# Routed experts of a decoder layer: every token times all experts, against slots sorted by expert in DRAM

## The chip, the core and the metric

The kernel runs on one core of one Trainium2 chip, in one launch. The metric is the device time of that core in microseconds (us), lower is better. The profile calls TensorE PE (its weight loads PEld), VectorE DVE, ScalarE ACT, GpSimd POOL and the queue that issues most DMAs SP.

## What is computed

2048 tokens (16 tiles of 128) of width 256 pass causal self-attention, cross-attention and a feed-forward stage, each behind a layer norm and added to `x`. Only the last stage changes. Its core, cut:

```python
shared = _swiglu(flat @ w_in.T) @ w_out.T                 # hidden width 512
g_idx = jnp.argmax(g_probs, axis=-1)                      # one of 2 groups of 4 experts
masked = jnp.where(g_idx[:, None] == egid[None, :], e_logits, -jnp.inf)
p_expert = _softmax(masked) * g_prob
topv, topi = jax.lax.top_k(p_expert, 2)                   # 2 of 8 experts for each token
w_se = zeros((S, 8)).at[arange(S)[:, None], topi].add(topv)
h = _swiglu(flat @ w1.T)                                  # the same h for all experts
routed = 0
for e in range(8):
    routed = routed + h * w_se[:, e:e + 1] @ w2[e].T      # 512 -> 256 for each expert
out = x + shared + routed
```

## The kernel before

All products are float32 by three matmuls of halves rounded to float32r (`product`, lines 118 to 124): high by low, high by high, low by high, summed in PSUM. So each operand exists as `_hi` (made by ACT with a copy) and `_lo` (the rest, by DVE or POOL: `weights_lo_pool`). The weights come through three staging buffers `stage`, loaded by SP; a load waits until the `_lo` of the piece three before it is done.

Two blocks follow each other, with a barrier of all engines between them. The first holds both attentions. The second is the feed-forward stage, over four groups of four token tiles (`TPG`), a rolled loop from the second on. For each group, TensorE does: `gate_logits`; `hidden(g)`, eight units of 12 matmuls of 512 columns (four for `w1`, four for `win`; "unit" below), the first four with hidden rows on the partitions, so that they can be the weights side later; and `outputs(g)`: for each token tile four chunks (two experts each, 12 matmuls of 512 columns), that is every token times all eight experts, and one chunk `wout` (12 matmuls of 256 columns). ACT makes silu and the high halves, DVE the product `h` with the gate half and the low halves, and in `combine` the weighted sum over the experts with the weights `wse` of `gating(g)` (zero for the six not chosen). `combine` follows the matmuls chunk by chunk through four PSUM banks `OB`; a finished tile goes out by one DMA.

```python
for c in range(OUTS):                       # 5 chunks: 4 pairs of experts, 1 shared
    ...
    for k in range(HT):
        ...
        mm = product(dst, lhs, rhs, k == 0, k == HT - 1)
    mm.then_inc(out_mm, 1)
```

## Time and profile before

| | |
|---|---|
| median of 3 runs | 955.28 us (953.64 to 955.29) |
| profiled execution, first to last instruction | 953.4 us |
| TensorE busy | 929.8 us, 98% |
| second block (feed-forward), from about | 649.3 us |
| its TensorE busy time to the end | 294.65 of 304.1 us |
| granted TensorE clock, mean | 0.996 |

The profiled execution has no time of its own beside its span; the median of the runs is 1.9 us above that span. Times in the rows are us from the span's start, durations of one instruction are in ns where a row says mean. The program's own copy of the line numbers is used: L122 to L124 are the three matmuls of `product`, so groups are told apart by their tiles.

### The profile page before, as it was taken

How to read it: one execution, taken by the hardware profiler on the slowest of the kernel's cores; microseconds unless marked ns; L12 is line 12 of the kernel's file. 1: busy time of each engine (PE TensorE's matmuls, PEld its weight loads, DVE VectorE, ACT ScalarE, POOL GpSimd, SP SyncE). 2: the span in 40 equal slices, each digit the busy share in tenths (PEclk: the TensorE clock that was granted, in tenths of full speed). 3: DMA queues.
4: the chain of work that ended last, by engine and by line, in shares of the span. 5: the costliest groups of instructions: out<-in, count | busy, mean ns of one | idle time of the engine just before them, and what ended most of it. 6: DMA issues, size and time to landing. Idle time of an engine off the chain costs nothing. (4 is left out here: it accounts for less than half of the span.)

```text
span 953.4 us, 17962 instructions
## 1 busy us (share of the span) xinstructions
PE 929.8 (98%) x6242; PEld 798.4 (84%) x6242; DVE 629.0 (66%) x1630; ACT 518.1 (54%) x1603; POOL 231.4 (24%) x243
## 2 busy tenths in 40 slices
PE   7999999999999989999999999997999999999998
PEld 5788889888888878988988988886788888888887
DVE  5787778687688777767667766766843653553543
ACT  4876677667667767766766777776301400400400
POOL 0443124124115344512421522435000000000000
PEclk9999999999999999999999999999999999999999
DMA  7200000000001020000000020112000000000000
GB/s 230 102 23 2 1 0 0 0 0 0 0 1 46 23 67 2 23 2 0 0 22 0 0 88 0 46 45 103 8 12 12 0 11 11 0 11 11 1 11 12
DMA packets 13184, 22.07 MB, mean 23 GB/s; under 512 B 1108, under 2 KB 7764, under 8 KB 12628
## 3 DMA queue, kind: packets, MB, share of 16 engines
q1 hardware_dynamic: 13140, 21.51, 6.9%
q8 instruction: 25, 0.41, 0.2%
q14 instruction: 19, 0.16, 0.1%
HBM read 19.41 MB, written 2.10 MB: 23 GB/s over the span
## 5 line engine op out<-in xcount | busy, mean ns | idle before, releaser
L383 POOL TENSOR_TENSOR prob<-prob,rsum 128x512 f32<-128x512 f32 x128 | 133.2, 1040 | 395.2 <-DVE rsum L576 395.2
L461 ACT ACTIVATE prob<-psS,nmin 128x128 f32<-128x128 f32 x512 | 180.9, 377 | 6.1 <-DVE nmin L560 3.5
L444 ACT ACTIVATE pT_hi<-psT 128x512 fp32r<-128x512 f32 x128 | 69.5, 595 | 85.9 <-PE psT L715 85.9
L461 ACT ACTIVATION_READ_ACCUMULATOR prob<-psS,nmin 128x1 f32 x512 | 111.6, 218 | 0.0
L545 DVE TENSOR_TENSOR oT_lo<-psT,oT_hi 64x512 fp32r<-64x512 f32 x128 | 88.0, 688 | 22.5 <-ACT oT_hi L449 20.5
L539 DVE TENSOR_TENSOR pT_lo<-psT,pT_hi 128x512 fp32r<-128x512 f32 x128 | 82.1, 682 | 1.6 <-ACT pT_hi L444 1.4
L449 ACT ACTIVATE oT_hi<-psT 64x512 fp32r<-64x512 f32 x128 | 75.8, 592 | 5.2 <-PE psT L124 3.6
L533 DVE TENSOR_TENSOR v_lo<-psW,v_hi 128x512 fp32r<-128x512 f32 x64 | 44.2, 690 | 50.5 <-ACT v_hi L439 50.5
L122 PE MATMUL psT<-pT_lo,v_hi 128*128 128x256 f32 x256 | 72.8, 284 | 4.6 <-DVE pT_lo L539 4.6
L439 ACT ACTIVATE v_hi<-psW 128x512 fp32r<-128x512 f32 x64 | 38.2, 597 | 68.5 <-PE psW L124 68.5
L703 PE MATMUL psS<-kt_lo,q_hi 64*128 64x128 f32 x512 | 73.7, 285 | 0.0
L122 PE MATMUL psA<-wo_lo,oT_hi 128*128 128x256 f32 x256 | 72.8, 284 | 0.8 <-DVE oT_lo L545 0.8
L124 PE MATMUL psT<-pT_hi,v_lo 128*128 128x256 f32 x256 | 72.6, 283 | 0.0
L123 PE MATMUL psA<-wo_hi,oT_hi 128*128 128x256 f32 x256 | 72.4, 283 | 0.0
L123 PE MATMUL psT<-pT_hi,v_hi 128*128 128x256 f32 x256 | 72.3, 283 | 0.0
L124 PE MATMUL psA<-wo_hi,oT_lo 128*128 128x256 f32 x256 | 72.2, 282 | 0.0
L560 DVE CUSTOM_DVE_ANT_0 psS<-psS,mask 128x128 f32<-128x128 f32 x256 | 65.4, 325 | 9.1 <-PE psS L703 8.6
L715 PE MATMUL psT<-ident,prob 128*128 128x128 f32 x512 | 69.9, 280 | 0.8 <-DVE oT_lo L545 0.8
L703 PE MATMUL psS<-kt_hi,q_lo 64*128 64x128 f32 x512 | 70.4, 272 | 0.0
L703 PE MATMUL psS<-kt_hi,q_hi 64*128 64x128 f32 x512 | 70.3, 271 | 0.0
L703 PEld LDWEIGHTS psS<-kt_lo,q_hi 64*128 64x128 f32 x512 | 48.6, 187 | 17.9 <-issue 15.7
L576 DVE RECIPROCAL rsum<-psums 128x4 f32<-128x4 f32 x128 | 22.0, 172 | 57.3 <-ACT prob L461 57.3
(196 smaller groups left out, 2595.0 us busy)
## 6 DMA issues: line engine op xcount, KB each, us to landing
stage<-w SPq DMA_DIRECT2D x4, 1024.0 KB, 4.8
stage<-ctxT SPq DMA_DIRECT2D x4, 512.0 KB, 4.1
out<-fin SPq DMA_DIRECT2D x16, 128.0 KB, 1.7
xres<-x SPq DMA_DIRECT2D x3, 512.0 KB, 8.3
stage<-wq SPq DMA_DIRECT2D x2, 512.0 KB, 5.3
stage<-wk SPq DMA_DIRECT2D x2, 512.0 KB, 6.6
stage<-wv SPq DMA_DIRECT2D x2, 512.0 KB, 5.4
stage<-wr SPq DMA_DIRECT2D x2, 512.0 KB, 5.0
```

The costliest lines, as they stand in the source:

```text
L122: nc.tensor.matmul(o, lh, rl, start=start, stop=False, **kw)
L123: nc.tensor.matmul(o, lh, rh, start=False, stop=False, **kw)
L124: return nc.tensor.matmul(o, ll, rh, start=False, stop=stop, **kw)
L383: nc.gpsimd.tensor_tensor(prob[:, r, :], prob[:, r, :], rsum[:, r].unsqueeze(2).broadcast_to([P, TPG, P]), ALU.mult).then_inc(prob_done, 1)
L444: nc.scalar.activation(pT[0][:, i, :], psT[:, i, :], ACT.Copy).then_inc(pT_hi, 1)
L449: nc.scalar.activation(oT[0][r, parity, :, :], banks(psT)[r, :, h, :], ACT.Copy).then_inc(oT_hi, 1)
L461: e = nc.scalar.activation(prob[:, n, :], flat(psS[:])[:, n * P:(n + 1) * P], ACT.Exp, bias=nmin[:, n:n + 1], scale=-1.0, accum_out=psums[ ...
L539: nc.vector.tensor_tensor(pT[1][:, i, :], psT[:, i, :], pT[0][:, i, :].bitcast(F32), ALU.subtract).then_inc(pT_lo, 1)
L545: nc.vector.tensor_tensor(oT[1][r, parity, :, :], banks(psT)[r, :, h, :], oT[0][r, parity, :, :].bitcast(F32), ALU.subtract).then_inc(oT_l ...
L560: m = nc.vector.tensor_tensor_reduce(sc, sc, mask[:], 1.0, LARGE, ALU.add, ALU.min, nmin[:, i * TPG + n:i * TPG + n + 1])
L703: mm = nc.tensor.matmul(psS[:, h, c], lhs[r, c], rhs[r, c], start=n == 0, stop=n == 2, skip_group_check=True)
L715: mm = nc.tensor.transpose(psT[:, i, n * P:(n + 1) * P], prob[:, i * TPG + n, :], ident[:])
```

## The change

The 2048 tokens times 2 choices are sorted by expert. A slot is a row of a DRAM tensor `hs` (4992 rows of 512 float32); each expert owns whole tiles of 128 slots, so there are at most `NT` = 39 tiles, and each has one expert.

- The `w1` units are now made by token tile with the token on the partition (units `H0` to `H15`, again 12 matmuls of 512 columns each), and `h` stays in the staging buffers. The `win` units are `S00` to `S33`. Both use the PSUM pairs `psS` and `psT` in turn; unit u waits until DVE has done unit u-2.
- The gate weights are worked out for groups 0 to 2 together and then for group 3 (`gate_maxima`, `gate_ranks`). `slot_counts` (17 small matmuls) and `slots` give each token its two slots; `slot_experts` gives each tile its expert.
- POOL issues 32 indirect DMAs that scatter `h` (128 rows of 2 KB each) to `hs`. `hs` is set to zero in the first block by one DMA of 10.2 MB. SP waits for all scatters and loads the tiles back, six in flight.
- For each of the 39 tiles TensorE transposes 128x512 (`turn`), ACT and DVE make the halves, TensorE loads the expert's column offset into a register (`value_load`) and does 12 matmuls of 256 columns (`expert`); ACT copies the result and SP writes it to `ys`.
- When all of `ys` is written, POOL issues 32 indirect DMAs that gather 128 rows of 1 KB each, through twelve buffers, and DVE adds them with their weights to `xres` (`add_routed`), which goes out.
- Order on TensorE: `H` and `S0` units with gates in between, the other `H`, `S10` to `S13`, `S20`, `shared_out(1)`, the 39 tiles, then `S21` to `S33` with `shared_out(2)`, at last `shared_out(3)`.
- The six late weight pieces of up to 1 MB are now ten: `w2` comes in eight of 512 KB, seven of whose low halves POOL makes.

```diff
+NT = (CHOICES * B * S + NE * (P - 1)) // P
+LOADS = 6
+YGS = 12
+BUFS = 3
...
+                sp.dma_start(hs.rearrange("(t p) d -> p t d", p=P),
+                             zero[:].unsqueeze(1).broadcast_to([P, NT, HID])).then_inc(slots_zero, 16)
...
             @block2.sync
...
+                for n in range(REUSED):
+                    sp.wait_ge(scattered[n], 2 * CHOICES * 16)
+                sp.wait_ge(scattered_rest, (HSLOTS - REUSED) * CHOICES * 16)
+
+                def load_slots(i):
+                    if i >= LOADS:
+                        sp.wait_ge(hT_mm, i - LOADS + 1)
+                    sp.dma_start(hl(i), hs[i * P:(i + 1) * P, :]).then_inc(hl_in[i % LOADS], 16)
+
+                for i in range(LOADS):
+                    load_slots(i)
+                for i in range(NT):
+                    if i + LOADS < NT:
+                        load_slots(i + LOADS)
+                    sp.wait_ge(y_copied, i + 1)
+                    sp.dma_start(ys[i * P:(i + 1) * P, :], y_rows(i)).then_inc(y_out[i % BUFS], 16)
...
             @block2.gpsimd
...
+                late_lo(LATE.index("win"))
+                ln_scale(pool, L0 + 2)
...
+                pool.wait_ge(slots_zero, 16)
+                pool.wait_ge(slots_known, 1)
+                for T in range(B):
+                    u = UNITS.index(f"H{T}")
+                    pool.wait_ge(h_done, u + 1)
+                    for c in range(CHOICES):
+                        d = nc.gpsimd.indirect_dma_start(
+                            hs[:, :], bass.IndirectOffsetOnAxis(ap=slot[:, c, T:T + 1], axis=0), h_slot(T), None,
+                            bounds_check=SLOTS - 1, oob_is_err=False)
...
+                for b in range(BUFS):
+                    pool.wait_ge(y_out[b], (NT // BUFS) * 16)
+                for n in range(B * CHOICES):
+                    if n >= YGS:
+                        pool.wait_ge(added, n - YGS + 1)
+                    nc.gpsimd.indirect_dma_start(
...
             @block2.scalar
...
+                def expert_hi(i):
+                    act.wait_ge(hT_mm, i + 1)
+                    if i >= BUFS:
+                        act.wait_ge(y_mm, i - BUFS + 1)
+                    nc.scalar.activation(flat(hT(0, i)), T_BANKS[i % BUFS], ACT.Copy).then_inc(hT_hi, 1)
+
+                def copy_rows(i):
+                    act.wait_ge(y_mm, i + 1)
...
+                    nc.scalar.activation(y_rows(i), Y_BANKS[i % BUFS], ACT.Copy).then_inc(y_copied, 1)
...
             @block2.vector
...
+                for i in range(NT):
+                    dve.wait_ge(hT_hi, i + 1)
+                    nc.vector.tensor_tensor(flat(hT(1, i)), T_BANKS[i % BUFS], flat(hT(0, i)).bitcast(F32),
+                                            ALU.subtract).then_inc(hT_lo, 1)
...
+                def add_routed(T):
+                    dve.wait_ge(shared_added, 2 * (T // TPG + 1))
+                    for c in range(CHOICES):
+                        n = T * CHOICES + c
+                        dve.wait_ge(yg_in[n % YGS], 16 * (n // YGS + 1))
...
+                        nc.vector.scalar_tensor_tensor(xres[:, T, :], yg(n), weight[:, c, T:T + 1], xres[:, T, :],
+                                                       ALU.mult, ALU.add).then_inc(added, 1)
...
             @block2.tensor
...
+                def turn(i):
+                    pe.wait_ge(hl_in[i % LOADS], 16 * (i // LOADS + 1))
...
+                    for k in range(HT):
+                        tr = nc.tensor.transpose(T_BANKS[i % BUFS][:, k * P:(k + 1) * P], hl(i)[:, k * P:(k + 1) * P], ident[:])
+                    tr.then_inc(hT_mm, 1)
+
+                def expert(i):
+                    offset = pe.value_load(offsets[0:1, i:i + 1], min_val=0, max_val=(NE - 1) * D)
+                    pe.wait_ge(hT_lo, i + 1)
...
+                    for k in range(HT):
+                        mm = product(Y_BANKS[i % BUFS], (hT(0, i)[:, k, :], hT(1, i)[:, k, :]),
+                                     tuple(w[:, k, bass.ds(offset, D)] for w in w2s), k == 0, k == HT - 1)
+                    mm.then_inc(y_mm, 1)
...
+                turn(0)
+                turn(1)
+                for i in range(NT):
+                    if i + 2 < NT:
+                        turn(i + 2)
+                    expert(i)
```

TensorE, before: the end of one token tile of `outputs`. The first three rows are the last products with a pair of experts, 512 columns; the next three begin the shared part, 256 columns.

```order
L122 MATMUL psT<-w2_lo,hid_hi 128x512
L123 MATMUL psT<-w2_hi,hid_hi 128x512
L124 MATMUL psT<-w2_hi,hid_lo 128x512
L122 MATMUL psA<-wout_lo,hid_hi 128x256
L123 MATMUL psA<-wout_hi,hid_hi 128x256
L124 MATMUL psA<-wout_hi,hid_lo 128x256
```

TensorE, after the change: the end of `shared_out(1)` and the first expert tile (`stage` holds the loaded slots, `w1_hi` and `w1_lo` hold the halves of the transposed rows).

```order
L143 MATMUL psA<-wout_hi,hid_lo 128x256
L1478 MATMUL psS<-ident,stage 128x128 x8
L1478 MATMUL psW<-ident,stage 128x128 x4
L1482 TENSOR_LOAD offsets
L1482 ISA x2
L141 ISA
L141 MATMUL psT<-w2_lo,w1_hi 128x256
L142 REGISTER_ALU
L142 MATMUL psT<-w2_hi,w1_hi 128x256
L143 MATMUL psT<-w2_hi,w1_lo 128x256
```

The 48 matmuls of 512 columns for each token tile are gone; in their place stand, 39 times, 4 transposes, one register load with 10 register instructions (the last five rows come four times), and 12 matmuls of 256 columns.

POOL, before, from its first low half in the second block to the end; its last three instructions are a loop over the layer norms.

```order
L257 TENSOR_TENSOR win_lo<-stage,win_hi 128x2048
L257 TENSOR_TENSOR w2_lo<-stage,w2_hi 128x2048 x2
L883 UNCONDITIONAL_BRANCH
L883 ISA
L150 TENSOR_TENSOR veps<-mv,eps 128x4
L152 TENSOR_TENSOR rstd<-veps,mhalf 128x4
```

POOL, after the change, from the same place (`wq_lo` is where the low half of `win` now goes) to the end.

```order
L277 TENSOR_TENSOR wq_lo<-stage,wq_hi 128x2048
L169 TENSOR_TENSOR veps<-mv,eps 128x4
L171 TENSOR_TENSOR rstd<-veps,mhalf 128x4
L277 TENSOR_TENSOR w2_lo<-stage,w2_hi 128x1024 x2
L169 TENSOR_TENSOR veps<-mv,eps 128x4
L171 TENSOR_TENSOR rstd<-veps,mhalf 128x4
L277 TENSOR_TENSOR w2_lo<-stage,w2_hi 128x1024 x5
L1012 DMA hs<-stage,slot 4992x512 x32
L1022 DMA stage<-ys,slot 128x256 x32
```

POOL, which had nothing to do behind its low halves but four small operations for each layer norm, now ends with 64 DMAs that it issues itself.

DVE, before: the end of its program, the last token tile of `combine`.

```order
L1022 SCALAR_TENSOR_TENSOR fin<-psA,wse,fin 128x256
L1022 SCALAR_TENSOR_TENSOR acc<-psA,wse,acc 128x256
L1026 TENSOR_TENSOR acc<-psA,acc 128x256
L1029 TENSOR_TENSOR fin<-fin,acc 128x256
```

DVE, after the change: the end of its program, from the last unit on.

```order
L1223 TENSOR_TENSOR silu<-psT,silu 128x512
L1228 TENSOR_TENSOR hid_lo<-silu,hid_hi 128x512 x2
L1366 SCALAR_TENSOR_TENSOR xres<-stage,weight,xres 128x256 x16
L1341 TENSOR_TENSOR xres<-psA,xres 128x512 x4
L1366 SCALAR_TENSOR_TENSOR xres<-stage,weight,xres 128x256 x16
```

All 32 additions of expert results now stand behind the last unit of the shared part.

## Rows read from the trace of the kernel before

**Rows 1.** The page, span and busy time of each engine.

```profile
span 953.4 us, 17962 instructions
PE 929.8 (98%) x6242; PEld 798.4 (84%) x6242; DVE 629.0 (66%) x1630; ACT 518.1 (54%) x1603; POOL 231.4 (24%) x243
```

**Rows 2.** Windows of the second block: busy of each engine, clock, DMA share, GB/s.

```profile
649.30:677.70 28.40, 22.22 (x88) 17.11 (x89) 23.48 (x20) 18.64 (x20) 14.36 (x5) 0.94 0.26 93
677.70:728.00 50.30, 50.30 (x250) 42.68 (x249) 27.56 (x76) 5.64 (x8) 1.21 (x2) 1.00 0.03 9
...
sum 304.10, PE 294.65 PEld 243.47 DVE 158.48 ACT 62.03 POOL 17.98; mean PE 36.83 PEld 30.43 DVE 19.81 ACT 7.75 POOL 2.25
```

**Rows 3.** Timeline of PE: start, length, instruction; from one token tile.

```profile
702.40 0.40 PE L122 MATMUL psA<-w_lo,hid_hi 128*128 128x512 f32 x1
...
713.30 0.28 PE L122 MATMUL psA<-wout_lo,hid_hi 128*128 128x256 f32 x1
...
714.74 1.04 PE L172 MATMUL psS<-ident,z 128*128 128x128 f32 x8
715.53 0.48 PE L122 MATMUL psA<-w_lo,hid_hi 128*128 128x512 f32 x1
```

**Rows 4.** Timeline of PE, two pieces of a score step with 64x128 matmuls.

```profile
212.39 0.27 PE L703 MATMUL psS<-kt_hi,q_lo 64*128 64x128 f32 x2
212.50 0.27 PE L703 MATMUL psS<-kt_lo,q_hi 64*128 64x128 f32 x2
```

**Rows 5.** Groups of instructions from 660 us on: count, busy, mean ns.

```profile
L1022 DVE SCALAR_TENSOR_TENSOR fin<-psA,wse,fin 128x256 f32<-128x256 f32 x24 | 11.6, 482 | 30.3 <-PE psA L124 30.2
L992 DVE TENSOR_TENSOR h<-psS,silu 128x512 f32<-128x512 f32 x15 | 10.4, 692 | 19.2 <-ACT silu L896 19.0
L896 ACT ACTIVATE silu<-psW 128x512 f32<-128x512 f32 x15 | 9.0, 599 | 23.6 <-PE psW L124 23.6
L152 POOL TENSOR_TENSOR rstd<-veps,mhalf 128x4 f32<-128x4 f32 x3 | 3.0, 1007 | 0.2
```

**Rows 6.** Timelines of POOL and DVE while the weights come in.

```profile
655.84 4.62 POOL L257 TENSOR_TENSOR w_lo<-stage,w_hi 128x2048 fp32r<-128x2048 f32 x1
656.02 4.99 DVE L1002 TENSOR_TENSOR hid_lo<-h,hid_hi 128x512 fp32r<-128x512 f32 x1
664.52 0.68 DVE L992 TENSOR_TENSOR h<-psW,silu 128x512 f32<-128x512 f32 x1
```

**Rows 7.** DMAs: size and median us from issue to landing; SP's issues at the start.

```profile
out<-fin SPq DMA_DIRECT2D x16, 128.0 KB, 1.7
xres<-x SPq DMA_DIRECT2D x4, 128.0 KB, 2.2
0.82 1.83 SPq L338 DMA_DIRECT2D xres<-x  x4
```

**Rows 8.** Window in which weights load: DMA share and GB/s are the last two columns.

```profile
655.00:660.00 5.00, 5.00 (x23) 3.89 (x21) 4.59 (x2) 3.71 (x5) 5.00 (x2) 1.00 0.55 210
```

**Rows 9.** Timeline of DVE, the gate weights of the first group, first and last.

```profile
680.55 0.16 DVE L939 TENSOR_REDUCE gmax<-logits 128x4 f32<-128x8 f32 x1
...
683.18 0.43 DVE L965 TENSOR_TENSOR above<-probs 128x256 f32<-128x256 f32 x1
...
685.35 0.19 DVE L976 SCALAR_TENSOR_TENSOR wse<-rank,probs 128x32 f32<-128x32 f32 x1
```

**Rows 10.** Windows of gaps in TensorE's work; the clock is third from the end.

```profile
665.00:670.00 5.00, 3.06 (x12) 2.18 (x12) 4.90 (x3) 3.52 (x4) 4.07 (x1) 1.00 0.31 105
670.00:675.00 5.00, 4.53 (x13) 3.58 (x14) 4.50 (x5) 0.63 (x1) 0.00 (x0) 0.66 0.00 0
```

**Rows 11.** The end, by timelines: last instruction of PE, DVE and SP.

```profile
949.86 0.28 PE L124 MATMUL psA<-wout_hi,hid_lo 128*128 128x256 f32 x1
950.63 0.42 DVE L1029 TENSOR_TENSOR fin<-fin,acc 128x256 f32<-128x256 f32 x1
951.23 0.33 SPq L870 DMA_DIRECT2D out<-fin  x1
```

More of the change, by code:

```diff
@@ new lines, in build, with s_before @@
+            ROUND = (range(0, 3 * TPG), range(3 * TPG, B))
+            UNITS = ["H0", "H1", "H2", "H3", "S00", "S01", "S02", "S03", "H4", "H5", "H6", "H7", "H8", "H9", "H10", "H11",
+                     "H12", "H13", "H14", "H15", "S10", "S11", "S12", "S13", "S20", "S21", "S22", "S23",
+                     "S30", "S31", "S32", "S33"]
+            S_UNITS = [n for n in UNITS if n[0] == "S"]
+            H_AFTER = ("w1 lower", "w1 upper", "win", "w2 2 upper", "w2 3 lower", "w2 3 upper")
+            def s_before(u):
+                return sum(n[0] == "S" for n in UNITS[:u])
@@ new lines, in _ @@
+                late_hi(4)
+                late_hi(5)
+                exps(0)
+                bias(3)
+                unit(9)
+                late_hi(6)
+                late_hi(7)
+                exps(1)
+                unit(10)
+                late_hi(8)
+                late_hi(9)
+                for u in range(11, UNITS.index("S10") + 1):
+                    unit(u)
+                for m in range(HT):
+                    unit(UNITS.index(f"S1{m}") + 1)
+                    split(f"S1{m}")
```

747 lines of the change are left out of this document (492 added, 255 removed).

## The prediction

> **What bounds the kernel now.** I read the page first, then windows over the second block, then TensorE's timeline inside a token tile, then the timelines of POOL and DVE where weights load. TensorE is busy for 98% of the span, DVE for 66%, POOL for 24% [rows 1]. In the second block TensorE works 294.65 of 304.1 us [rows 2], so the reader should see that this stage is bound by the number of matmul columns alone. The idle 9.4 us are in the first group (28.4 us, 22.2 busy) and behind the last matmul. Within a token tile the rows follow each other without a gap: from the first product with an expert pair to the first shared one 10.90 us pass for 48 matmuls of 512 columns, 0.227 us each; the 12 of 256 columns take 1.44 us, and 8 transposes 0.79 us [rows 3]. DVE keeps up with room to spare: in the steady window it is busy 27.6 of 50.3 us.
>
> **What is removed.** The experts' products: 16 tiles times 10.90 us = 174.4 us, all on the path.
>
> **What is added on TensorE.** Each of the 39 expert tiles has 12 matmuls of 256 columns (1.44) and 4 transposes (half of 0.79, so 0.40): 1.84 us, 71.8 in all. The 32 units, the 16 shared products, the gate products and the transposes of z are as many as before, only in another order. The 17 small matmuls of the slot counts are about 0.1 each by the transposes, less than 2 us with the first one's wait: I take 1. If nothing ever waits, the span is 953.4 - 174.4 + 71.8 + 1 = 851.8 us. Everything else is what has to be given back.
>
> **The register load in each expert tile.** The trace has no load of a register on TensorE. It blocks TensorE's sequencer, with 10 register instructions behind it. What hides it is that the sequencer runs ahead: matmuls of 128 columns are issued each 0.055 us (two in 0.11 [rows 4]), while one of 256 columns lasts 0.12, so a tile lets it gain 12 times 0.065 plus a little on the transposes, about 1.0 us. Against that stand the register instructions, at 0.05 each by the same row 0.5 us, and the load. Lower bound: all hidden, 0. Upper bound: the nearest round trip through memory in the trace, a small store's 1.7 us [rows 7], gives 0.5 + 1.7 - 1.0 = 1.2 us for a tile, 47 in all. Between them I take 0.4 for a tile, that is a load of 0.9, shorter than a DMA because nothing is written: +15.6 us. The Trainium skill, DMA: Bandwidth & Descriptors, in Latency and other measured facts, gives a floor of about 600 ns for such a load. As an estimate by that page the loop would give back 39 times 0.1, some 4 us; no row here shows it.
>
> ACT and DVE don't bind the loop: ACT has a copy of 512 columns, 0.6 us, and one of 256, DVE one low half read from PSUM, 0.69 like the product [rows 5], against 1.84 to 2.3. The pair runs two tiles ahead, 3.7 us, and takes about 1.6. The DMAs have 256 KB in and 128 KB out for a tile. At a DMA share of 0.55 the trace moved 210 GB/s [rows 8], so about 380 GB/s is there, and 393 kB need 1.0 us. They are hidden too, by the same 1.84 us.
>
> **The scatters.** The price of one indirect DMA on POOL, c, is the term that decides, and the trace has none: POOL issues no DMA there. Lower bound: SP issues one of 128 rows in 1.83 / 4 = 0.46 us [rows 7]. Upper bound: if each were to wait for the one before to land, 1.7 to 2.2 us [rows 7]. POOL's own rows say that even a computed power on 4 columns takes it 1.0 us [rows 5]; making 128 descriptors in software is nearest to that, and I take c = 1.25.
>
> The slots are known when DVE is through `slots`. I placed it by walking the program: TensorE then has H10 to H15, S10 to S13 and S20 before it, 11 units of 2.72, and `shared_out(1)`, 5.76, with a wait of 1 us for the chain of small DVE operations: 36.7 us of cover. The scatters need 32 c, one landing (2.2) and the first load (2.2): 44.4 us. So TensorE stands 7.7 us before the first transpose. Behind a gap the granted clock falls: after 5 us in which TensorE worked 3.1 it was 0.66 over the next 5 [rows 10], 1.7 us of work lost. Together +9.4 us. With c at 0.46 the wait is nothing, at 2.2 it is 38.
>
> **The gates, earlier.** The gate chain of one group takes 5 us on DVE, its operations of 256 columns 0.43 [rows 9]. For twelve tiles the five big ones have 768 columns, about 0.95 each, so the chain is some 8 us, between units H4 and H5 of DVE. `shared_out(0)`, 5.76, and two units of double buffering cover it. The low half of `win` is now queued on POOL behind the layer norm of group 1 and seven constants, so S00 waits for it some 3 us; ACT and DVE come late by another 4 around the staged weights. A low half with both operands in SBUF stretches to 4.99 us when POOL is making one of weights (4.62), while the product that reads PSUM stays at 0.68 beside it [rows 6]; in the new order the H units read PSUM, and only S00 to S03 are exposed. This is 7 to 8 us of waits where the first group had its own 6 [rows 2] and the rest is in the terms above: net 0, between -4 and +8.
>
> **The seams.** Filling the transpose pipeline 1.5 us, the last copy of the experts 0.6: +2.1. Behind S33, silu, product and two halves (0.6 + 0.7 + 0.6 + 0.7 and their signals) stand before `shared_out(3)` with nothing left to cover them: +3.
>
> **The gathers.** All the additions stand behind S33's low half. 12 gathers are done by then: from the last write of `ys` there are 25 us of units and `shared_out(2)`. The other 20 each wait for an addition to free a buffer, and are issued one after the other: 20 c = 25 us. With the first addition 0.5, the landing 2.2, the last additions and signal 1.1 and the last store 2.2 [rows 5, 7], the kernel ends 31.0 us after S33. TensorE would be done 5.8 us after it. Before, 3.3 us lay between TensorE's end, 950.1, and the span's [rows 11]. So +21.9 us. `shared_out(3)` and `add_shared` lie under it.
>
> **Sum.** 851.8 + 15.6 + 9.4 + 0 + 2.1 + 3 + 21.9 = 903.8 us of span. The median of the runs is 1.9 above the span of the profiled execution, so 905.7; I say **905 us**, 5% faster. Of what is saved on TensorE, half comes back as waits.
>
> The memory side costs nothing at the start: the 10.2 MB of zeros need about 27 us at 380 GB/s, behind the loads of the first attention and far ahead of the next pieces. If a load did queue behind them, it would be one wait of that size; I see none.
>
> **Rivals.**
>
> *POOL's DMAs cost 1.8 us or more.* Each 1 us of c costs 32 in front and 20 behind, 52 us. At c = 1.8 it is 934, at 2.2 it is 955, level; beyond 2.25 the change is slower. This is the case that ends on the other side, with POOL as the engine that everything waits for, and the place would be the gap before the first transpose and the tail. For it: POOL is slow in everything, 1.0 us for 4 columns and 4.6 for 2048 [rows 5, 6]. Against it: descriptors are 128, not 65536 elements. The Trainium skill, DMA: Bandwidth & Descriptors, Anatomy of one DMA, puts a DMA from this engine at about 2.0 us and its bytes over 436 GB/s, by estimate 2.6 us for a scatter and 2.3 for a gather. Were these in series, the time would be about 970 by the same estimate; the page lays most of the 2 us on the landing, which does not hold the next issue, and no row here shows either. Chance 0.22, of which 0.09 slower.
>
> *The expert tiles run at 3 us.* The register load stalls the sequencer in full, 1.2 us for a tile: 47 - 15.6 = +31, so 937. For it: a blocking instruction in a stream that issues ahead. Against: the 1.0 us that the sequencer gains. Chance 0.13.
>
> *Gathers and additions hold each other up.* The additions read two operands in SBUF, and [rows 6] show such an operation standing still for POOL's work. If each of 20 gathers also waits for an addition (0.48 [rows 5]), +10 us: 915. The Trainium skill, SBUF — State Buffer, Who interferes with whom, says that a DVE instruction with two SBUF inputs contends with a GpSimd instruction that reads SBUF, which [rows 6] bear out, but that descriptors need the write side, so that they would not be held. Chance 0.15.
>
> *Cheap DMAs and a hidden load.* c near 0.6 and no loss in the loop: the front wait is gone (-9.4), the tail has 12 (-13), the loop gives -15.6: 867. Chance 0.12.
>
> The forecast itself, c from 1.0 to 1.6 and 0.2 to 0.7 a tile, has 0.38 and spans 885 to 925. The range over all that leaves out no more than 2 in 10 is 872 to 948. A measurement tells about 0.2% from no change. Faster than that 0.88, within it 0.03, slower 0.09.
>
> **What would show it.** TensorE's routed matmuls fall from 174 us to about 56. The 39 tiles start 2.2 to 2.4 us apart, 1.84 if the load is hidden. POOL's issues in a row stand 1.25 us apart, and TensorE's longest wait is before the first transpose, 5 to 12 us. After TensorE's last matmul some 25 us pass with only POOL, DVE and DMAs. The prediction is wrong if POOL's issues stand over 2 us apart, if the tiles stand over 3 us apart, or if the units before the slots lose more than 10 us to ACT, DVE and the staged weights.

## The result and the profile after

The changed kernel took 945.03 us (median of 4 runs, 941.11 to 945.92) beside 955.28 for the kernel before: ratio 0.9885, 95% interval 0.986 to 0.9909, so 1.2% faster. Forecast were 905 us, from 872 to 948. The profiled execution has a span of 939.3 us where the sum had 903.8: 35.5 us more. In a later session (the fourth of those below) the same kernel took 916.62 us (ratio 0.9612, 0.9577 to 0.9647), with a span of 914.0: the kernel before was at 954 to 955 us in every session, this one was not. Most of the experiments below are about that difference.

The page of the kernel after, against [rows 1]:

```profile
span 939.3 us, 17987 instructions
...
PE 851.3 (91%) x6115; PEld 741.0 (79%) x6115; DVE 596.2 (63%) x1513; ACT 546.3 (58%) x1667; POOL 304.0 (32%) x318
...
L1022 POOL DMA_INDIRECT stage<-ys,slot x32 | 32.6, 1017 | 128.1 <-DMA ys<-z 99.7
...
stage<-hs SPq DMA_DIRECT2D x39, 256.0 KB, 2.9
...
ys<-z SPq DMA_DIRECT2D x39, 128.0 KB, 1.9
```

TensorE's work fell by 78.5 us, but its share of the span fell too, from 98% to 91%. Windows tell where; they end at the first scatter, the first expert product, the end of the loop, and S33's low half. The busy columns are PE, PEld, DVE, ACT, POOL. First the execution of 939.3 us:

```profile
649.30:726.30 77.00, 60.05 (x276) 47.43 (x277) 56.24 (x123) 33.40 (x44) 25.93 (x21) 0.88 0.14 48
726.30:793.20 66.90, 44.28 (x196) 35.21 (x195) 16.91 (x33) 11.23 (x20) 31.37 (x32) 0.83 0.41 153
793.20:870.50 77.30, 75.93 (x613) 72.28 (x614) 26.00 (x38) 36.55 (x75) 0.00 (x0) 1.00 0.56 175
870.50:902.20 31.70, 26.98 (x132) 22.64 (x131) 9.04 (x15) 7.93 (x14) 12.19 (x12) 0.95 0.18 54
902.20:939.30 37.10, 7.34 (x48) 7.17 (x48) 17.00 (x37) 0.00 (x0) 20.37 (x20) 0.59 0.43 128
```

Then the same kernel in the later session:

```profile
649.30:724.80 75.50, 59.64 (x272) 46.92 (x273) 55.00 (x122) 32.16 (x43) 25.89 (x21) 0.88 0.14 49
724.80:774.50 49.70, 42.73 (x199) 35.60 (x198) 17.65 (x33) 11.50 (x20) 31.73 (x32) 0.91 0.55 206
774.50:849.90 75.40, 74.82 (x611) 73.00 (x610) 25.59 (x37) 36.37 (x75) 0.00 (x0) 0.98 0.60 179
849.90:881.00 31.10, 25.66 (x133) 21.33 (x132) 9.18 (x15) 8.31 (x15) 12.17 (x12) 0.99 0.19 55
881.00:914.00 33.00, 8.58 (x48) 8.41 (x48) 16.86 (x36) 0.00 (x0) 20.45 (x20) 0.60 0.49 144
```

The second stretch, in which POOL issues the 32 scatters, is 17.2 us longer in the first measurement: 22.6 us without TensorE at work against 7.0. The last one is 4.1 us longer; together these two are 21.3 of the 25.3 us between the sessions. The prediction's own chain, read backwards (903.8 less 31.0, 29, 87.4 and 46), has the first scatter at 710.4, the first expert product at 756.4, the loop's end at 843.8 and S33's low half at 872.8. (87.4 is the loop, 71.8 + 15.6; 46 is 36.7 + 7.7 and the filling of the pipeline; 29 is about 25 of units, 0.6 and 3.)

What stands still in the second stretch is seen on two engines. TensorE's last matmuls of the units H13, H14 and H15, in the timeline of the kernel after:

```profile
738.76 0.39 PE L143 MATMUL psT<-w_hi,zlo 128*128 128x512 f32 x1
...
741.79 0.39 PE L143 MATMUL psS<-w_hi,zlo 128*128 128x512 f32 x1
...
749.60 0.40 PE L143 MATMUL psT<-w_hi,zlo 128*128 128x512 f32 x1
763.04 0.79 PE L141 MATMUL psS<-z_lo,wq_hi 128*128 128x512 f32 x1 [13.04 <-issue]
```

ScalarE's silus of H13, H14, H15 and S10:

```profile
744.14 0.60 ACT L1036 ACTIVATE silu<-psT 128x512 f32<-128x512 f32 x1 [5.76 <-remote]
761.66 0.60 ACT L1036 ACTIVATE silu<-psS 128x512 f32<-128x512 f32 x1 [16.92 <-remote]
768.74 0.60 ACT L1036 ACTIVATE silu<-psT 128x512 f32<-128x512 f32 x1 [6.48 <-PE psS L143]
769.23 0.59 ACT L1036 ACTIVATE silu<-psS 128x512 f32<-128x512 f32 x1
```

H14's products are done at 742.2, and its silu starts at 761.66, 19.5 us later; H12's is 1.4 us late, H13's 5.0, H15's 18.8 and S10's 0.7. In the other units this distance is 0.04 us, but for the first and for H6 (5.0 and 6.1), which are the same in the later session. Such a silu waits for two semaphores: TensorE's count of units and VectorE's count of products, and the second was there (VectorE did H12's product at 738.42). The trace's record of semaphores (it tells when each was raised) has TensorE's update for H14 at 761.64: the signal itself comes late, while the matmuls go on. "remote" says just that: no instruction ended near the update. S10, two units on, then waits until VectorE has done H14's product, at 762.98: TensorE's gap of 13 us. Meanwhile POOL issues a scatter each 1.28 us, until it too has to wait for the products of H14 (1.7 us) and H15 (4.8 us):

```profile
739.35 0.97 POOL L1012 DMA_INDIRECT hs<-stage,slot  x1 [0.30 <-issue]
740.62 0.97 POOL L1012 DMA_INDIRECT hs<-stage,slot  x1 [0.30 <-issue]
```

Ahead of the slots, that is before the first scatter, VectorE has the gates of twelve tiles beside POOL's low halves (timelines of DVE, then POOL):

```profile
694.73 2.47 DVE L1159 TENSOR_TENSOR logits<-logits,emax 128x96 f32<-128x96 f32 x1
...
700.58 0.96 DVE L1190 TENSOR_TENSOR above<-probs 128x768 f32<-128x768 f32 x1
...
706.98 2.38 DVE L1200 TENSOR_SCALAR unsel<-rank 128x96 f32<-128x96 f32 x1
...
694.65 4.81 POOL L277 TENSOR_TENSOR w_lo<-stage,w_hi 128x1024 fp32r<-128x1024 f32 x2 [9.67 <-ACT w_hi L268]
```

And in the tail `shared_out(3)` waits for `add_shared(2)`, which VectorE has behind 16 additions, and `add_shared(3)` for the signal of `shared_out(3)` (ended at 920.2, by the record of semaphores told 6.0 us later, at 926.2). Behind it POOL stands too, for a free buffer:

```profile
912.83 0.55 PE L141 MATMUL psA<-wout_lo,hid_hi 128*128 128x256 f32 x1 [13.30 <-DVE xres L1341]
...
902.20 7.11 DVE L1366 SCALAR_TENSOR_TENSOR xres<-stage,weight,xres 128x256 f32<-128x256 f32 x14
...
911.40 1.28 DVE L1341 TENSOR_TENSOR xres<-psA,xres 128x512 f32<-128x512 f32 x2
926.21 1.29 DVE L1341 TENSOR_TENSOR xres<-psA,xres 128x512 f32<-128x512 f32 x2 [13.52 <-remote]
...
928.66 1.09 POOL L1022 DMA_INDIRECT stage<-ys,slot  x1 [4.46 <-DVE xres L1366]
```

In the later session the same signal comes 0.02 us behind its matmul, and POOL's 20 gathers run from 882.1 to 908.3 without a stop. There TensorE's wait before the first transpose is the one that was forecast:

```profile
770.68 1.69 PE L1478 MATMUL psS<-ident,stage 128*128 128x128 f32 x8 [3.11 <-DMA stage<-hs]
```

### The profile page after: what moved, and what is told of

Its sections match the earlier page's. It is cut to its first block and busy times, and to the rows that moved or that the text cites. A ratio compares the mean times of both kernels' runs of the same rounds, so it can differ in the third digit from the quotient of the medians.

```text
span 939.3 us, 17987 instructions
## 1 busy us (share of the span) xinstructions
PE 851.3 (91%) x6115; PEld 741.0 (79%) x6115; DVE 596.2 (63%) x1513; ACT 546.3 (58%) x1667; POOL 304.0 (32%) x318
## 5 line engine op out<-in xcount | busy, mean ns | idle before, releaser
L481 ACT ACTIVATE pT_hi<-psT 128x512 fp32r<-128x512 f32 x128 | 69.6, 595 | 85.6 <-PE psT L752 85.6
L141 PE MATMUL psT<-pT_lo,v_hi 128*128 128x256 f32 x256 | 73.1, 285 | 4.6 <-DVE pT_lo L576 4.6
L1022 POOL DMA_INDIRECT stage<-ys,slot x32 | 32.6, 1017 | 128.1 <-DMA ys<-z 99.7
```

The lines of the kernel that those rows point to most:

```text
L141: nc.tensor.matmul(o, lh, rl, start=start, stop=False, **kw)
L481: nc.scalar.activation(pT[0][:, i, :], psT[:, i, :], ACT.Copy).then_inc(pT_hi, 1)
```

## The experiments

Theory: TensorE's signals are held up while POOL issues DMAs in a long unbroken row. Rivals: DMA traffic as such; something in TensorE's own instruction stream; a tail that is as long as its gathers, whatever the order. Each group below ran on one chip in one session; ratios are to the kernel before, beside it. The kernel after itself was measured in the first measurement and in the fourth session only, so a time beside its 945.03 us or its trace of 939.3 us is a comparison across sessions; whether a signal is late is read inside each trace.

### First session: order of the tail, pauses, plain stores

*tail_shared_first*

```diff
+                add_shared(2)
                 for T in range(B):
-                    if T == 2 * TPG:
-                        add_shared(2)
+                    if T == TPG + 1:
                         add_shared(3)
                     add_routed(T)
```

> Only the order of VectorE's tail changes: add_shared(2) comes ahead of the first routed addition and add_shared(3) behind those of five token tiles. Theory 1 (the tail is held by its order): TensorE no longer stands 13.3 us before shared_out(3), which ends near 908 instead of 920, VectorE's idle 13.5 us before add_shared(3) go, and what is left is 20 gathers of 1.3 us from 903.4: the span falls by 5 to 8 us, to about 933. Theory 2 (the gathers alone hold the tail): the wait of TensorE goes and the end stays within 2 us of 939.

942.46 us, 0.9863 (0.9828 to 0.9897), not told apart from the kernel after. From S33's low half to the end it has 34.1 us instead of 37.1; TensorE still waits 4.1 us, since the shared addition stands behind S33's halves, and the signal of `shared_out(3)` is 2.8 us late. Theory 2 comes nearer in that the wait of TensorE shrinks and little is won. But part of the 37.1 us is the late signal: where it is absent, in the fourth session, the unchanged order takes 33.0 us.

*adds_between*

```diff
+                    if name == "S32":
+                        add_shared(2)
+                    if name in ("S30", "S31", "S32", "S33"):
+                        add_routed(next(routed))
+                        if name != "S33":
+                            add_routed(next(routed))
```

> VectorE does the routed additions of the first seven token tiles between the units S30 to S33, so that POOL need not stop after twelve gathers; add_shared(2) stands behind unit S32. Theory 1 (the tail is as long as the gathers that start late): 32 gathers run from 872.8 at 1.3 us each to about 915, the last landing, addition and store end near 920: 19 us less than 939. Theory 2 (gathers and additions disturb each other, or TensorE's units are delayed by the additions on VectorE): the units S30 to S33 lose 5 us or more and the end is at 926 or later. Theory 3 (a run of gathers without a stop delays what TensorE signals, as seems to happen during the scatters): silu of some unit after about 882 starts several us after its matmuls have ended.

935.12 us, 0.9797 (0.9768 to 0.9826). From the last expert product to the kernel's end 61.2 us instead of 69.6: 8 of the 19 expected. Gathers ran in one row of 16 up to 896.7. Behind its thirteenth, TensorE stands for "issue" in the middle of `shared_out(2)`, waiting for nothing, and its clock falls to 0.50; the same in S31, whose silu comes 18.3 us behind S30's (12.3 in the kernel after):

```profile
893.39 0.28 PE L142 MATMUL psA<-wout_hi,hid_hi 128*128 128x256 f32 x1
...
894.51 0.38 PE L143 MATMUL psA<-wout_hi,hid_lo 128*128 128x256 f32 x1 [0.84 <-issue]
...
896.63 0.28 PE L143 MATMUL psA<-wout_hi,hid_lo 128*128 128x256 f32 x1 [1.12 <-issue]
```

Near theory 3, but stronger than it said: beside a long row of gathers not only TensorE's signals are late, its instructions are held too. The additions are not slowed by it, at 0.51 us each.

*scatter_pauses*

```diff
+                    if T % 2 == 1:
+                        if T % HSLOTS < REUSED:
+                            pool.wait_ge(scattered[T % HSLOTS], (T // HSLOTS + 1) * CHOICES * 16)
+                        else:
+                            pool.wait_ge(scattered_rest, (T - REUSED + 1) * CHOICES * 16)
```

> After every second token tile POOL waits until its scatters have landed, some 1.5 us, eight times. In the kernel after, ScalarE's silu of H13 to H15 starts 5, 19 and 19 us after the last matmul of its unit, while POOL issues scatters without a stop. Theory 1 (a long unbroken row of software DMAs holds back TensorE's signals): with the pauses no silu starts more than 2 us late, the scatters take 41 + 12 us, and the first expert product comes at about 786 instead of 793: 3 to 8 us less. Theory 2 (the traffic itself holds them back, whatever the pauses): the lateness stays and the time grows by 3 to 12 us.

937.27 us, 0.9826 (0.9802 to 0.985). With eight pauses of 2.2 us added it is no slower: theory 1. The nine silus from H12 to S20 start 0.04 us after their matmuls; TensorE does H12 to S20 without a gap. What a pause costs, in POOL's timeline:

```profile
730.29 0.97 POOL L1012 DMA_INDIRECT hs<-stage,slot  x1 [0.30 <-issue]
733.79 0.97 POOL L1012 DMA_INDIRECT hs<-stage,slot  x1 [2.53 <-DMA hs<-stage,slot]
```

2.53 us instead of 0.30. First expert product at 791.2.

*plain_stores*

```diff
-                        d = nc.gpsimd.indirect_dma_start(
...
+                        sp.dma_start(hs[n * P:(n + 1) * P, :], h_slot(T)).then_inc(
```

> The 32 scatters are issued by SyncE as plain stores of the same bytes to consecutive rows, from the same moment on (the routed part of the output is therefore not the reference's). It tells the bytes from the software queue. Theory 1 (the software DMAs of POOL hold back TensorE's signals): silus of H12 to H15 are on time, 32 issues take some 15 us, the first expert product comes at 762 to 768 and the span is about 910. Theory 2 (DMA traffic out of SBUF does it): the same lateness of 5 to 19 us between TensorE's last matmul of a unit and its silu appears here, and the time falls by under 15 us.

917.73 us, 0.9627 (0.9606 to 0.9648), no silu late. SyncE had all 32 issued 21 us after the slots: theory 1. The gathers are POOL's as before, and behind their row the signal of `shared_out(3)` is 5.4 us late in this very execution. So 32 stores of the same bytes, issued by SyncE, do not bring it, and POOL's row does, in one and the same execution.

### Second session: length of the row, bytes, POOL beside the gates

*pauses_each_8*, the edit of scatter_pauses with

```diff
-                    if T % 2 == 1:
+                    if T % 4 == 3:
```

> As scatter_pauses, but a pause only after every fourth token tile, three in all. With eight pauses no signal of TensorE was late, the scatters took 56.8 us instead of some 41 to 47, that is 2.2 us for a pause, and SyncE's loads waited for them. Theory 1 (what matters is the length of the unbroken row; the first late signal came some 8 to 10 us after the row's start): eight scatters, 10.2 us, are just short enough, lateness stays under 2 us, the scatters end near 774 instead of 782.7, the first expert product comes at 780 to 784, and the span falls by 7 to 10 us to about 926. Theory 2 (each pause only makes up for lateness in proportion): late signals of 3 us or more are back and the time is that of scatter_pauses or higher.

929.38 us, 0.9732 (0.9705 to 0.9758). No silu late, scatters from 727.4 to 775.3, first expert product at 783.8, and now TensorE's wait is the one that the prediction had, for the scatters:

```profile
start us, us, engine line op out<-in xcount [idle before <-releaser]
779.96 1.94 PE L1483 MATMUL psS<-ident,stage 128*128 128x128 f32 x8 [11.69 <-DMA stage<-hs]
```

*tiny_scatters*

```diff
-                            hs[:, :], bass.IndirectOffsetOnAxis(ap=slot[:, c, T:T + 1], axis=0), h_slot(T), None,
+                            tiny[:, :], bass.IndirectOffsetOnAxis(ap=slot[:, c, T:T + 1], axis=0), h_slot(T)[:, 0:TINY], None,
```

> Each of the 32 scatters moves rows of 64 bytes instead of 2 KB, to a small tensor of their own, so that hs stays zero (the routed part of the output is therefore left out in effect). The number of software DMAs, their descriptors and their row are as before, the bytes are a 32nd. Theory 1 (number and density of POOL's DMAs delay TensorE's signals): silus of H14 to S10 start 4 to 25 us after their matmuls' end, as in the kernel after. Theory 2 (bytes, some 200 GB/s out of SBUF over the software queue): no silu is more than 1 us late, the units run through, and the first expert product comes at 775 or before.

(`TINY` is 16.) 943.78 us, 0.9896 (0.9862 to 0.993), as slow as the kernel after in the first measurement. At 6 GB/s of scatters in place of some 200, ScalarE's silus of H13, H14 and H15 give the same picture:

```profile
738.16 0.60 ACT L1038 ACTIVATE silu<-psT 128x512 f32<-128x512 f32 x1 [2.77 <-PE psT L145]
746.66 0.60 ACT L1038 ACTIVATE silu<-psS 128x512 f32<-128x512 f32 x1 [7.90 <-remote]
767.03 0.60 ACT L1038 ACTIVATE silu<-psT 128x512 f32<-128x512 f32 x1 [19.78 <-remote]
```

Theory 1: the row of POOL's DMAs brings it, and their bytes don't matter.

*quiet_pool*

```diff
-                            late_lo(LATE.index(f"w2 {k} {half}"))
+                            weights_lo_pool(pool, N0 + i, lo[:, 0:1, 0:64], hi[:, 0:1, 0:64])
...
-                                     tuple(w[:, k, bass.ds(offset, D)] for w in w2s), k == 0, k == HT - 1)
+                                     tuple(w[:, k, bass.ds(offset, D)] for w in (w2s if k == 0 else (w2s[0], w2s[0]))),
```

> POOL makes only 64 of 1024 columns of five late low halves of w2 (w2 1 lower to w2 3 lower), and the expert products take the high half in place of the low one for those rows (so the routed part is computed with other numbers). It tells what POOL's weight work costs VectorE in the gates. Theory 1 (an operation of VectorE with both operands in SBUF stands still beside such POOL work): the chain of gate_ranks for twelve tiles shrinks from 15.0 us to about 8.5, that of group 3 from 6.2 to 4.2, the first scatter is issued 8 to 10 us earlier, and the span falls by 6 to 9 us. Theory 2 (the chain is long by the number of its operations): the first scatter moves by less than 3 us and the time stays within 2 us.

933.88 us, 0.9782 (0.9747 to 0.9816). The first scatter is issued at 719.2 instead of 726.3 (726.5 to 727.4 in the three other kernels of the second session). The two operations that took 2.47 and 2.38 us are the first and the last of these rows:

```profile
694.20 0.39 DVE L1161 TENSOR_TENSOR logits<-logits,emax 128x96 f32<-128x96 f32 x1
...
700.54 0.96 DVE L1195 TENSOR_TENSOR ties<-ties,earlier 128x768 f32<-128x768 f32 x1
...
703.64 0.20 DVE L1202 TENSOR_SCALAR unsel<-rank 128x96 f32<-128x96 f32 x1
```

From `gmax` to the end of `wse` the chain has 10.3 us, 2.0 of them a wait for ScalarE, instead of 15.3: theory 1. The operations of 768 columns were 0.96 all along.

*combined* has the pauses after every fourth tile and every eighth gather, the additions between the units, and `add_shared(0)` ahead of S11:

```diff
+                    if n % 8 == 7:
+                        pool.wait_ge(yg_in[n % YGS], 16 * (n // YGS + 1))
...
+                BETWEEN = {"S23": 1, "S30": 4, "S31": 1, "S32": 1}
...
+                    for _ in range(BETWEEN.get(name, 0)):
+                        add_routed(next(routed))
+                    if name == "S30":
+                        add_shared(2)
```

> Pauses after every fourth token tile of scatters and after every eighth gather; VectorE adds the shared part of group 0 before unit S11 instead of behind S13, does seven token tiles of routed additions between the units S23 to S33, and add_shared(2) behind unit S30. If a long row of software DMAs is what delays TensorE's signals and the late start of 20 gathers is what makes the tail: first expert product at about 780, gathers without a wait for buffers, 32 of them in 42 us and three pauses of 2.2, the end 54 us after the first gather instead of 66.5: the span is near 914, between 908 and 920. If the two do not add up (additions and gathers disturb each other): 921 or more.

919.19 us, 0.9616 (0.9589 to 0.9643), with a span of 917.7. From the first gather to the end 56.7 us instead of 66.5: a little above the 54 expected. Rows of eight gathers don't end the lateness: the silus of S31 and S32 start 1.9 and 2.1 us behind their matmuls, where those beside the scatters start after 0.04:

```profile
882.52 0.60 ACT L1043 ACTIVATE silu<-psT 128x512 f32<-128x512 f32 x1 [11.62 <-remote]
885.47 0.60 ACT L1043 ACTIVATE silu<-psS 128x512 f32<-128x512 f32 x1 [1.83 <-remote]
```

### Third session: register loads, plain DMAs of POOL, low halves on VectorE

*const_offset*

```diff
-                    offset = pe.value_load(offsets[0:1, i:i + 1], min_val=0, max_val=(NE - 1) * D)
+                    offset = i % NE * D
```

> The kernel after, but each expert tile takes its column offset from a constant (i mod 8) and loads no register; the routed part is thus made with other experts. In the kernel after, 39 tiles take 76 to 77 us, 1.95 each, where the matmuls alone count 1.84. Theory 1 (the load is hidden by the sequencer's lead but for a tenth of a us): the tiles come down to 1.84 to 1.88 us and the loop to 72 to 73.5, 3 to 4.5 us less. Theory 2 (the 0.1 us is the copies', the signals' or the transposes'): the loop stays within 1.5 us of 76. Against the prediction's 0.4 a tile, 15.6 us, both would speak.

915.42 us, 0.9591 (0.957 to 0.9611). This was not expected by either theory: no silu was late beside 32 scatters without a pause, so the loss of the second stretch was gone in a kernel that differs only behind it. (From the first expert product to the end of the last 72.3 us pass instead of 76.4: theory 1.) Hence the fourth session.

*pool_plain*

```diff
-                        d = nc.gpsimd.indirect_dma_start(
...
+                        d = pool.dma_start(hs[n * P:(n + 1) * P, :], h_slot(T))
```

> The kernel after, but POOL issues the 32 scatters as plain stores of the same 256 KB each to consecutive rows, so nothing is indirect (the routed part is not the reference's). It tells the indirect form from the engine that issues. Theory 1 (any unbroken row of DMAs issued by POOL delays TensorE's signals): silus of H14 to S10 are 4 to 25 us late as in the kernel after. Theory 2 (only the indirect form, whose addresses POOL reads and works out, does it, or a pitch as short as 1.3 us): no silu is over 1 us late, and the first expert product comes before 776.

913.27 us, 0.957 (0.9552 to 0.9588), no silu late. POOL issued 26 such DMAs in 14.1 us, 0.54 each. As no kernel measured beside it shows late signals, it does not tell the indirect form from POOL's plain DMAs. That stays open.

*combined_lows*, beside combined

```diff
                 gate_maxima(0)
+                late_lo(4)
+                late_lo(5)
                 gate_ranks(0)
...
-                    if T % 4 == 3:
+                    if T in (3, 7):
```

> The combined kernel with two more edits: VectorE makes the five low halves of w2 1 lower to w2 3 lower itself, between the parts of the gates and behind slots, 1.22 us each, instead of POOL beside them at 2.4; and POOL pauses only after token tiles 3 and 7, so that its last row has 16 scatters. In the kernel with a quiet POOL the first scatter came 7.2 us earlier; four of the halves, 4.9 us, now stand ahead of the slots and one of 1.22 is moved behind. Theory 1 (sum of both): first scatter 3.5 us earlier, scatters 2.2 shorter, the span 4 to 7 us below the combined kernel's 917.7, at 911 to 914. The signal of shared_out(1), inside the row of 16, comes several us late, and costs nothing, since the transposes wait for the scatters anyway. Theory 2: the late signal holds VectorE's low halves of the experts and the gain of the pause is lost, or the halves on VectorE cost TensorE as much as they give the gates: within 2 us of 917.7.

911.1 us, 0.9559 (0.9531 to 0.9588), span 906.8. First scatter at 718.1 instead of 726.9: 8.8 us earlier, more than the 3.5 of theory 1 (721.9, so 5.0 us, when it ran again in the fifth session). No signal was late here, so the expected delay of `shared_out(1)` didn't show; it did in the fifth session, by 7.2 us, hidden as expected behind the wait for the scatters.

### Fourth session: is it the register loads or the session?

*after_again* is the kernel after, unchanged; *const_again*, the edit of const_offset, and *one_load* stand beside it:

```diff
+                    if i == 0:
+                        loaded = pe.value_load(offsets[0:1, i:i + 1], min_val=0, max_val=(NE - 1) * D)
+                    offset = loaded if i == 0 else i % NE * D
```

> The kernel after, unchanged, beside the next one on one chip. The kernel with constant offsets had no late signal of TensorE at all in 32 scatters without a pause, and was 26 us faster, though it was changed only behind the scatters. Theory 1 (the register loads further on in TensorE's stream have to do with the late signals): this kernel shows them again, silus of H13 to S10 up to 20 us late, and takes some 943 us. Theory 2 (they depend on the chip or on the moment): here they are absent or small, and it takes 915 to 922 us, the kernel with constant offsets less by only 3 to 5 us.

> The kernel with constant column offsets once more (the routed part is made with other experts), beside the unchanged kernel. Theory 1 (register loads): no late signals, about 915 us, 25 to 30 us less than the unchanged kernel beside it. Theory 2 (chip or moment): the two kernels show the same late signals, or both none, and differ by the loop alone, 3 to 5 us.

> Constant offsets in all expert tiles but the first, which still loads its offset into a register (the routed part is made with other experts). If the register loads matter at all: by one (something static in the stream) the late signals are back, about 940 us; by their number, they are absent, about 915. If it is the chip or the moment, this goes with the two others of the call.

916.62 us, 0.9612 (0.9577 to 0.9647); 914.93 us, 0.9571 (0.9542 to 0.96); 914.82 us, 0.9573 (0.9545 to 0.9602). None has a late signal. ScalarE's silus of H12 to H14 in the unchanged kernel, beside 32 scatters in one row:

```profile
735.03 0.60 ACT L1036 ACTIVATE silu<-psS 128x512 f32<-128x512 f32 x1 [2.15 <-PE psS L143]
737.75 0.60 ACT L1036 ACTIVATE silu<-psT 128x512 f32<-128x512 f32 x1 [2.12 <-PE psT L143]
740.48 0.60 ACT L1036 ACTIVATE silu<-psS 128x512 f32<-128x512 f32 x1 [2.12 <-PE psS L143]
```

Register loads are out as the cause: theory 2. The loop has 75.4 us with 39 loads, 73.1 without and 71.7 with one: 2 to 4 us for all of them. The session had the chip number of the second one, so the late signals don't go by that number alone either.

*no_pauses* is combined_lows without its pauses:

```diff
-                    if T in (3, 7):
...
-                    if n % 8 == 7:
-                        pool.wait_ge(yg_in[n % YGS], 16 * (n // YGS + 1))
```

> The combined kernel with the low halves on VectorE and no pauses at all, register loads as in the kernel after. Theory 1 (late signals from register loads together with a long row): silus of H13 and later up to 20 us late, first expert product at 780 or later instead of 772.5, more than 911 us. Theory 2 (chip or moment): where the unchanged kernel beside it shows no late signals neither does this, and without the pauses it is 4 to 8 us faster than 911, at 903 to 907.

897.83 us, 0.9399 (0.9374 to 0.9425), span 896.4: the fastest kernel, 6% below the one before, and below the 903 to 907 expected.

### Fifth session: the best two again, unchanged, as no_pauses_b and combined_lows_b

> The fastest kernel so far (combined edits, low halves on VectorE, no pauses) once more in another session, for the late signals of TensorE that appeared in three sessions and not in two others. Theory 1 (they depend on the session, whatever the kernel): if they are here, the silus of H13 and later start up to 20 us late and the time is 910 to 925; if they are not, it is 896 to 900 as before. Theory 2 (this kernel is free of them by its build): 896 to 900 in any session, even if the kernel's profile of a session with the disturbance would show it.

> The same with two pauses among the scatters and one after every eighth gather, beside it. Where the late signals are absent it is 11 to 14 us slower than without pauses, as in the sessions before (911 against 898), since each of the five pauses costs 2.2 us. Where they are present it is the faster of the two, at 911 to 914.

The same kernel without pauses took 926.84 us here, 0.9711 (0.9684 to 0.9738), and the one with pauses 912.28 us, 0.9559 (0.9535 to 0.9583). The late signals are back in the first, here for H14, H15 and S10:

```profile
736.23 0.60 ACT L1035 ACTIVATE silu<-psS 128x512 f32<-128x512 f32 x1 [2.68 <-PE psS L143]
747.44 0.60 ACT L1035 ACTIVATE silu<-psT 128x512 f32<-128x512 f32 x1 [10.61 <-remote]
765.64 0.60 ACT L1035 ACTIVATE silu<-psS 128x512 f32<-128x512 f32 x1 [17.60 <-remote]
```

So theory 1, and theory 2 (a build free of it) falls. Without pauses the kernel is 13 us faster where the signals are on time (897.8 and 911.1, in two sessions of that kind) and 15 us slower where they are not; with them the time is nearly the same in both cases, 911 and 912.

## Why the prediction was right and wrong

Right in direction and within its range, wrong in size: a gain of 1.2% where 5% were forecast. The span was 35.5 us above the sum in the first measurement, 10.2 in the fourth session; the late signals are most of what lies between. That 945 us fell into the range owes something to luck: the range was made for dearer scatters and loads, and neither came. By its steps, first against the trace of 939.3 us and, in brackets, against 914.0:

- **The scatters, price.** The price of one, c = 1.25, was right: issues stand 1.28 us apart, gathers 1.30. The rival with 1.8 and more is out; so are "cheap DMAs" for the indirect form. The Trainium skill, DMA: Bandwidth & Descriptors, Anatomy of one DMA, gives 2.0 us and the bytes' share for one DMA and lays most of it on the landing. The trace agrees: the pitch is 1.28, and a pause that waits for the landing adds 2.2.
- **The scatters, the cover ahead.** This is the step that failed: "TensorE stands 7.7 us before the first transpose", with 36.7 us of units as cover. It took for granted that the units run through beside the scatters. From first scatter to first expert product 66.9 us [49.7] passed where the prediction's numbers give 46: +20.9 [+3.7]. TensorE's signals were late; pauses and plain stores take the delay away, and it is absent in the fourth session. Of TensorE's 22.6 idle us 18.0 lay in front of H15, S10 and S11 and 3.3 before `shared_out(1)`, none before the transpose. Where the signals are on time, the step holds as it was meant: 3.7 us of waits before the first transposes, for the scatters' rows to come back, with 3.3 before `shared_out(1)`, which it had left out.
- **Slots known.** The first scatter was issued at 726.3 [724.8] where the prediction's chain has 710.4: +15.9 [+14.4], in both sessions. What failed here is "net 0" in "The gates, earlier". It took 8 us for the chain, and said that "only S00 to S03 are exposed" to POOL. The chain took 15.3, its small operations standing up to 2.2 us beside low halves of `w2`. With a quiet POOL the first scatter comes 7 us earlier. TensorE's units ahead of the scatters waited 5.7 us for `z` and 3.6 us for the logits; by the trace that is most of the rest, and no run takes it apart. The rule was in [rows 6] and was applied to the wrong operations.
- **The register load.** 15.6 us was mis-sized: tiles stand 1.95 us apart [1.93], the loads cost 2 to 4 us in all. The loop was 10.1 us shorter [12.0] than forecast. The load takes 0.3 to 0.6 us on the sequencer by the trace where 0.9 was taken; that the sequencer's lead hides nearly all of it fits the way of hiding that was forecast. The estimate by the Trainium skill, DMA: Bandwidth & Descriptors, Latency and other measured facts, with its floor of about 600 ns, was 4 us for the loop; the runs agree.
- **The seams and the chain behind S33.** 29 us from the loop's end to S33's low half, measured 31.7 [31.1]: +2.7 [+2.1], near.
- **The tail.** 31.0 us, measured 37.1 [33.0]: +6.1 [+2.0]. That 20 gathers set it was right: in the fourth session 1.2 us, a row of 26.2 us and 5.6 us behind it make 33.0, and `shared_out(3)`, in spite of its wait behind 16 additions and a granted clock of 0.60 over the stretch, did "lie under it". In the first measurement it didn't, because its signal was 6.0 us late: its addition, and with it POOL's 29th gather (4.5 us idle), waited for it. In the five other kernels with this tail in sessions with late signals the last stretch is 37.2 to 37.3 us, in the four others without them 32.8 to 32.9. The rival "gathers and additions hold each other up" did not come by its mechanism: additions take 0.5 us beside gathers.

Sum, in the order of time: +15.9 +20.9 -10.1 +2.7 +6.1 = +35.5 [+14.4 +3.7 -12.0 +2.1 +2.0 = +10.2]. No rival had the late signal.

Shown are: that the signal is late and not ScalarE or VectorE, that a long row of POOL's indirect DMAs and not their bytes brings it, that beside rows of eight scatters no silu is late (beside rows of eight gathers up to 2.5 us stay), and that it comes in some sessions (three of five, and the first measurement). One execution of each kernel has a trace; that the others of the same session have it too is concluded from their times, which agree within 0.7%. Not shown is what makes a session one kind or the other, where the signal is held, and whether plain DMAs of POOL would do it too.

A rival stands untested: the recording itself. Where none is missing, each DMA leaves 16 records of its landing. In all eleven traces of sessions with late signals records are missing beside POOL's rows, also where rows are broken by pauses and nothing is late: the gathers left 108 to 295 of 512, the indirect scatters 122 to 354. In the seven traces of the other sessions it is 510 to 512 and 512. SyncE's loads and stores in the expert loop, beside which POOL issues nothing, have at least 622 of 624 in every trace. Every execution here has its span and clock on record, so each was recorded; whether signals are late in one that isn't, no run shows.

## What to carry to other kernels

- TensorE's work is not sure cover for a long row of POOL's indirect DMAs: in four of six sessions TensorE's signals came late beside it. Give plain transfers to SyncE. Waits for a landing, 2.2 us each, two among the scatters and one after every eighth gather, kept the last kernel at 911 to 912 us, where without them it took 898 or 927; whether it pays depends on how often such sessions come.
- When work is moved beside POOL, list every VectorE operation with SBUF operands in that stretch, small ones first: two of them took 2.4 to 2.5 us here where 0.2 and 0.4 are due, as long as POOL's operation beside them.
- In a tail that runs at the pace of one engine's issues, start that row as early as its data allow and place its consumers between the units that are still left: in the fourth session, from the first gather to the end, 61.0 us became 48.1. And measure such a kernel in several sessions: its four runs agreed within 0.6% each time, and the sessions differed by 3%.

## What the runs showed of the hardware that was not expected

In executions that were all recorded, TensorE's semaphore updates came up to 19.5 us after the matmuls they belong to in the kernel after, and up to 24.6 in other kernels (adds_between). Beside scatters the matmuls kept their pace of 0.227 us meanwhile (H13 in the kernel after, H13 to H15 in adds_between); beside long rows of gathers there were gaps of 0.3 to 1.5 us inside chains of matmuls (adds_between, no_pauses_b). What waited for VectorE and ScalarE started on time: VectorE's products mostly 0.03 us behind ScalarE's silu, S10 0.06 us behind VectorE's product. The first late signal belongs to a unit that ended 10 to 11 us into the scatters' row (15 in no_pauses_b), and the backlog is gone within 5 us of the row's end. The bytes don't matter (64 against 2048 a row). The Trainium skill, SBUF — State Buffer, Who interferes with whom, says that a DMA never contends with a compute engine and that TensorE and ScalarE wait on no one. For the matmuls of H13 and H14 the trace agrees; for the signals, and for the chains beside the gathers, they don't, and there the measurement decides. The page speaks of SBUF's ports, and no run here shows where a signal is held.
